# Masking the chosen feed-forward blocks by GpSimd with gates loaded over DRAM, in place of a selector product on TensorE

## What is computed

```python
prob = softmax(xf @ router_w.T + router_b)
_, idx = top_k(prob, 4)
mask = zeros((n, 16), bool).at[arange(n)[:, None], idx].set(True)
h = einsum('nd,ibd->nib', xf, w1b) + b1b
h = relu(where(mask[:, :, None], h, 0))
y = einsum('nib,dib->nd', where(mask[:, :, None], h, 0.0), w2b) + b2
```

## Time and profile before

| | us |
|---|---|
| median of 3 runs | 829.46 (828.54 to 829.77) |
| the profiled execution | 827.81 |
| its span | 826.0 |
| PE busy | 812.7 |
| DVE busy | 576.8 |
| ACT busy | 426.3 |
| POOL busy | 284.2 |

### The profile page before, as it was taken

The page is one execution under the profiler, slowest core; times in us unless marked ns, Lnnn a source line. Parts: engine busy times, 40 slices in busy tenths (PEclk is TensorE's granted clock), DMA queues, the critical chain, the costliest instruction groups (busy, mean ns, idle before and its releaser), DMA issues.

```text
span 826.0 us, 14866 instructions
## 1 busy us (share of the span) xinstructions
PE 812.7 (98%) x5275; PEld 490.6 (59%) x5275; DVE 576.8 (70%) x1785; ACT 426.3 (52%) x1018; POOL 284.2 (34%) x301
## 2 busy tenths in 40 slices
PE   7999999999999999999999999999999999999998
PEld 3677454544556655656666556664766556465764
DVE  6879787787998766675786866667676776767312
ACT  3523555564645645554564554645565454546552
POOL 4494249343650158067041028509400002000000
PEclk9999999999999999999999999999999999999999
DMA  8952515232514253240333215232070415000011
GB/s 266 275 163 78 168 54 166 93 90 92 166 61 136 80 143 142 65 122 19 100 121 76 93 53 166 91 91 92 3 216 2 116 54 142 15 15 16 15 58 52
DMA packets 53335, 81.91 MB, mean 99 GB/s; under 512 B 6796, under 2 KB 22092, under 8 KB 53260
## 3 DMA queue, kind: packets, MB, share of 16 engines
q1 hardware_dynamic: 53260, 80.95, 32.4%
HBM read 43.06 MB, written 37.88 MB: 98 GB/s over the span
## 4 chain that ended last, share of the span: by engine, by line
PE 92%; DVE 4%; ACT 2%; issue 1%; DMA 1%; SPq 0%; ACTq 0%; DVEq 0%
PE o_bank L1149 16%; PE banks L1074 15%; PE banks L1133 14%; PE banks L1049 14%; PE banks L1062 14%; PE banks L1023 7%; PE banks L1136 3%; PE banks L1032 3%; PE banks L1101 3%; PE banks L1053 2%; ACT probs L950 2%; DVE part_max L1342 1%; PE banks L1013 1%; DMA bqk_sb<-in_bk 1%; DVE o_norm L1379 1%
## 5 line engine op out<-in xcount | busy, mean ns | idle before, releaser
L950 ACT ACTIVATE probs<-banks 128x512 f32<-128x512 f32 (+3 forms) x768 | 328.0, 496 | 243.8 <-PE banks L1136 174.4
L1133 PE MATMUL banks<-q_st,k_st 99*128 99x512 bf16 (+3 forms) x768 | 234.8, 327 | 2.6 <-ACT probs L950 1.0
L1074 PE MATMUL banks<-k_st,q_st 96*128 96x512 bf16 (+3 forms) x768 | 228.7, 327 | 0.6 <-DVE part_max L1342 0.2
L1345 DVE CUSTOM_DVE_ANT_0 banks<-banks,tri,part_max 128x512 f32<-128x512 f32 (+3 forms) x256 | 128.9, 556 | 68.3 <-PE banks L1074 67.9
L1342 DVE TENSOR_REDUCE part_max<-banks 128x1 f32<-128x512 f32 x256 | 160.0, 677 | 17.6 <-PE banks L1074 17.2
L1345 DVE CUSTOM_DVE_ANT_0 banks<-banks,tri 128x512 f32<-128x512 f32 (+3 forms) x256 | 120.0, 515 | 34.4 <-PE banks L1074 33.5
L836 POOL TENSOR_SCALAR max_neg<-row_max 128x16 f32<-128x16 f32 x32 | 8.2, 255 | 382.1 <-DVE row_max L1345 382.1
L1049 PE MATMUL banks<-xnT,w_sb 128*128 128x256 f32 x512 | 134.5, 386 | 0.1
L1149 PE MATMUL o_bank<-probs,v_sb 128*17 128x512 f32 (+3 forms) x1536 | 133.2, 487 | 0.7 <-DVE o_norm L1379 0.7
L1062 PE MATMUL banks<-w_sb,hT 128*128 128x256 f32 x512 | 121.2, 382 | 0.0
L1074 PEld LDWEIGHTS banks<-k_st,q_st 96*128 96x128 bf16 x768 | 73.4, 98 | 73.6 <-issue 19.6
(11 more groups left out here) (100 smaller groups left out, 734.3 us busy)
## 6 DMA issues: line engine op xcount, KB each, us to landing
term_scratch<-pieces SPq DMA_DIRECT2D x84, 256.0 KB, 2.8
q_st<-term_scratch SPq DMA_DIRECT2D x16, 768.0 KB, 6.0
k_st<-term_scratch SPq DMA_DIRECT2D x16, 768.0 KB, 8.4
y_scratch<-o_norm SPq DMA_DIRECT2D x31, 256.0 KB, 2.1
acc<-in_x SPq DMA_DIRECT2D x8, 512.0 KB, 4.0
rope_sb<-y_scratch SPq DMA_DIRECT2D x15, 256.0 KB
out<-acc SPq DMA_DIRECT2D x7, 512.0 KB, 2.9
x_sb<-in_x SPq DMA_DIRECT2D x3, 1024.0 KB, 5.9
```

Of the source, the lines that this page charges most:

```text
L950: nc.scalar.activation(probs[:, h, PROBS_AT[u]:PROBS_AT[u] + w], filled("score", n, k, h)[:, 0:w], ACT.Exp, scale=SCALE).then_inc(s_out, 1)
L1074: nc.tensor.matmul(bank[:, 0:w], q_st[0:KROWS, at, h, i * P:(i + 1) * P], k_st[0:KROWS, at, h, c * HALF:c * HALF + w], start=True, stop=Tr ...
L1133: last = nc.tensor.matmul(bank[:, 0:w], k_st[0:SROWS, at, h, j * P:(j + 1) * P], q_st[0:SROWS, at, h, q0:q0 + w], start=True, stop=not dia ...
L1345: ins = nc.vector.tensor_tensor_reduce(bank[:, 0:w], bank[:, 0:w], tri[:, HALF - w:HALF], 1.0, least, ALU.add, ALU.max, to)
```

## The change

In row 0 nothing changes in kind: the selector product stays, with `sel` and the mask now on 16 partitions instead of 128. In rows 1 to 3 the third matmul of `hidden` is left out. The mask (now called `chosen`, 1 for a chosen block) is transposed by PE as before, copied by DVE to `chosenT`, stored to DRAM (`store_chosen`), and read back with every block's row repeated over the 64 partitions of its hidden values into `gates` (`load_gates`, two DMAs for a quarter, a buffer each for even and odd quarters). GpSimd multiplies `hT` by `gates` in place, two m at a time (`gate`), and PE's `ffn_tile` waits on `gated` for each pair instead of on ACT. `sel` now lies in the second buffer of `gates` and the last group's output weights `wo_last` in `x_sb`, loaded in row 3 by one DMA from a prepared input instead of four at the start. The planner gets a cost for the gate (2700 columns), puts gates right behind splits in its priority, counts a hidden unit of rows 1 to 3 as a quarter-column product less, and holds an `ffn` part back until it thinks the gates are done.

```diff
-COST = {"hid": 2 * 4 * QTR + QTR, "ffn": FB // 2 * 4 * D, "proj": KB * 4 * HALF, "v": KB * 4 * (D + NBLK),
+COST = {"hid": 2 * 4 * QTR, "masked": 2 * 4 * QTR + QTR, "ffn": FB // 2 * 4 * D, "proj": KB * 4 * HALF, "v": KB * 4 * (D + NBLK),
...
+GATED, GATES = 500, 20000
-            todo = min(able, key=lambda todo: todo[1][0] != "split")
+            todo = min(able, key=lambda todo: ("split", "gate").index(todo[1][0]) if todo[1][0] in ("split", "gate") else 2)
+    def work_ready(what):
+        return what[0] != "ffn" or what[1] == 0 or gated.get((what[1], what[2] // 2, 2 * what[3] + 1), clock + 1) <= clock
...
+            def store_chosen(b):
+                if b >= 3:
+                    for buffer in range(2):
+                        sp.wait_ge(gates_in[buffer], (b - 2) * 2 * 32)
+                sp.wait_ge(m_out, M_COUNT["chosenT", b])
+                sp.dma_start(gate_scratch[b % 2], chosenT[:]).then_inc(chosen_out, 16)
+            def load_gates(b, q):
+                if b == 1 and q == 1:
+                    sp.wait_ge(s_out, S_COUNT["hid", 0, 3, FB - 1])
+                elif b > 1 or q > 1:
+                    sp.wait_ge(gated, (b * 4 + q - 5) * FB // 2)
+                if q == 0:
+                    sp.wait_ge(chosen_out, b * 16)
+                tokens = slice(q * QTR, (q + 1) * QTR)
+                for i in range(2):
+                    rows = gate_scratch[b % 2].rearrange("(m i) t -> i m t", i=2)[i, :, tokens]
+                    sp.dma_start(gates[i * 64:(i + 1) * 64, q % 2], rows.partition_broadcast(64)).then_inc(
+                        gates_in[q % 2], 16)
...
                 load_stacks(n + 2)
                 if b:
+                    store_chosen(b)
                     store_y(n - 1, 1)
                     load_y(b - 1, 1, 2, 4)
+                    load_gates(b, 0)
+                    load_gates(b, 1)
                 store_y(n, 0)
...
                 place_maxima(n + 1, 1)
+                if b:
+                    load_gates(b, 2)
                 store_y(n, 1)
...
                 place_maxima(n + 2, 1)
+                if b:
+                    load_gates(b, 3)
                 store_y(n + 1, 1)
...
+            def gate(b, q, pair):
+                pool.wait_ge(s_out, S_COUNT["hid", b, q, 2 * pair + 1])
+                if pair == 0:
+                    pool.wait_ge(gates_in[q % 2], (b * 2 + q // 2 - 1) * 32)
+                blocks = slice(2 * pair, 2 * pair + 2)
+                nc.gpsimd.tensor_tensor(hT[:, blocks, :], hT[:, blocks, :], gates[:, q % 2, blocks, :],
+                                        ALU.mult).then_inc(gated, 1)
...
-                nc.tensor.matmul(bank[:, 0:QTR], sel[:, m, :], unselT[:, tokens], start=False,
-                                 stop=True).then_inc(s_fill, 1)
+                if b == 0:
+                    if q == 0 and m == 0:
+                        pe.wait_ge(m_out, M_COUNT["chosenT", 0])
+                    last = nc.tensor.matmul(bank[:, 0:QTR], sel[:, m, :], chosenT[:, tokens], start=False, stop=True)
+                last.then_inc(s_fill, 1)
...
-                    if t % 2 == 0:
+                    if t % 2 == 0 and b == 0:
                         pe.wait_ge(s_out, S_COUNT["hid", b, t // 2, m])
+                    elif t % 2 == 0 and m % 2 == 0:
+                        pe.wait_ge(gated, (b * 4 + t // 2 - 4) * FB // 2 + m // 2 + 1)
```

More of the change, by code:

```diff
@@ L207 @@
 SPLIT, PLACE = 1200, 16000
-POOL = {"split": 3600, "sin": 5640, "cos": 5640, "add": 5640, "high": 2500, "rest": 5100, "mid": 2500,
+GATED, GATES = 500, 20000
+POOL = {"gate": 2700, "split": 3600, "sin": 5640, "cos": 5640, "add": 5640, "high": 2500, "rest": 5100, "mid": 2500,
         "low": 5100, "xn": 1580, "bias": 5700}
@@ L229, in arrange @@
     to_turn = [(n, half) for n in range(GROUPS) for half in range(2)]
+    gates = {}
     wide, values_free = True, 0
-    pool, pool_todo, pool_free, split = [], [], 0, {}
+    pool, pool_todo, pool_free, split, gated = [], [], 0, {}, {}
     def pool_work(ready, *works):
@@ L247, in pump @@
                 split[todo[1][1:]] = pool_free + SPLIT
+            elif todo[1][0] == "gate":
+                gated[todo[1][1:]] = pool_free + GATED
     def engine_of(kind):
@@ L317, in do_work @@
         what = works.pop(0)
+        while not work_ready(what):
+            clock += 50
+            pump()
         order.append(what)
@@ L324, in do_work @@
                 do_max()
-            order.append(works.pop(0))
+            what = works.pop(0)
+            while not work_ready(what):
+                clock += 50
+                pump()
+            order.append(what)
             clock += COST["ffn"]
             read(what, at, READ["ffn"])
+            wide = True
             return 2 * COST["ffn"]
-        read(what, fill(what, COST[what[0]]), READ[what[0]])
+        read(what, fill(what, cost(what)), READ[what[0]])
+        if what[0] == "chosenT":
+            gates[what[1]] = ready["vector"] + GATES
+        elif what[0] == "hid" and what[1] and what[3] % 2:
+            pool_work(max(ready["scalar"], gates.get(what[1], 0)), ("gate", what[1], what[2], what[3] // 2))
         if what[0] == "out" and what[1] + 1 < B and what[2] % 2:
@@ L336, in do_work @@
             chores.append((ready["scalar"] + FREED, scored + 9, ("found", what[1])))
-        return COST[what[0]]
+        return cost(what)
     def chore_ready():
@@ L393, in arrange @@
             do_max()
-        elif works:
+        elif works and work_ready(works[0]):
             do_work(works)
@@ L403, in arrange @@
             chores.extend((clock, scored + 2 * j + 2, what) for j, what in enumerate(steps))
-        total, done = sum(COST[what[0]] for what in works + [what for _, what in later]), 0
+        total, done = sum(cost(what) for what in works + [what for _, what in later]), 0
         for i in range(NU * GH):
@@ L421, in arrange @@
                     do_run()
-                elif may_work and done + COST[works[0][0]] / 2 <= share - SPARE:
+                elif may_work and done + cost(works[0]) / 2 <= share - SPARE:
                     if not wide and wide_max_ready():
@@ L490, in block_kernel @@
         tri_k = tri[:, HALF - P:HALF]
-        sel = sb("sel", [P, FB, P], BF16)
+        gates = sb("gates", [P, 2, FB, QTR], BF16)
         pieces = sb("pieces", [P, 2, NPIECE, T], BF16)
@@ L499, in block_kernel @@
         yT = rope_sb[:, 0]
-        wo_last = sb("wo_last", [P, D])
+        wo_last = x_sb[:, 0, :]
+        sel = gates[0:NBLK, 1, 0:FB // 2, :].rearrange("p a (c m) -> p (a c) m", m=P)
         o_norm = sb("o_norm", [P, 2, HALF])
@@ L877, in _ @@
             for what in POOL_ORDER:
-                if what[0] == "split":
+                if what[0] == "gate":
+                    gate(*what[1:])
+                elif what[0] == "split":
                     split_maxima(*what[1:])
@@ L1183, in _ @@
                     pe.wait_ge(wv_in, 32)
-                if what == ("unselT", 0):
+                if what == ("chosenT", 0):
                     pe.wait_ge(mask_in, 48)
@@ L1411, in take @@
             def take(what):
-                if what[0] == "unselT":
-                    take_unselected(*what[1:])
+                if what[0] == "chosenT":
+                    take_chosen(*what[1:])
                 elif what[0] == "ffn":
@@ L1493, in constants @@
     tri[:, HALF - P:] = np.where(np.arange(P)[None, :] > np.arange(P)[:, None], -BIG, 0.0)
-    sel = np.zeros((P, FB, P), np.float32)
+    sel = np.zeros((NBLK, FB, P), np.float32)
     for m in range(FB):
```

106 lines of the change are left out of this document (56 added, 50 removed).

## The result

The changed kernel takes 830.25 us (830.05 to 830.54, 15 runs), the kernel before 828.38 us (827.75 to 829.77, 15 runs) beside it: a ratio of 1.0022 [1.0015, 1.0029]. It is slower by 0.2%, where 1.0% faster was forecast.

A forecast was written before the change was run, and what follows sets the result against it. PE was taken to pace the kernel, with 92% of the chain. 827.81 - 10.3 (products) + 1.1 (late gate) + 0.6 (shorter filler) = 819.2 us, plus 1.65 to the runs' median: 820.9 us, 1.0% faster; range 817.5 to 826.5.

The forecast's parts named there:

- The price of a product: PE, rows 1 to 3: each removed selector product holds PE about 0.107 us, so 96 save 10.3 us.
- Row 0 keeps its 32: Row 0's selector products: reading 16 partitions instead of 128 costs nothing, since the count of columns is the same.
- its weight load lies beside other matmuls: PE, selector product: its weight load overlaps other matmuls, so nothing was counted for it.
- Between nothing and half of the saving I take that 6%: 0.6 us: Evictions on DVE or ACT: with hidden units as shorter filler, 0.6 us of the saving is given back.
- rival (a): PE's saving turns into waits for evictions, the new order having less filler: half of 10.3 us goes, 825.4 us; chance 0.18.
- The order now keeps the same units: Between last hidden unit and tile: distances stay but for 0.1 to 0.3 us, so eleven tiles' gates cost nothing.
- The gates: GpSimd, 48 gates of 1.07 us (upper bound 1.18): PE waits once, row 1 quarter 3 pair 3, 1.1 us.
- rival (d): DVE slows beside GpSimd's gates, which read two SBUF operands: 26 us on DVE, half on the chain, 832 us; chance 0.03.
- Quarter 2's rotary steps: GpSimd, quarter 2: `add` and `high` stand ahead of pairs 2 and 3; gate 3 still ends about 1.4 us before its reader.
- The last tile of all: Smallest distance from ACT's write to the tile's read, 2.4 us; at least 0.7 us left after the gate.
- SyncE, the DMAs and the splits: Added loads and stores hidden, gates ahead of splits harmless: nothing counted; range allows 0 to 2 and 0 to 3 us.
- what would show it: Trace signs: 32 selector products, PE busy near 803 us, one `hT` wait; wrong if DVE and ACT's chain share grows over 1%.

## Why the prediction was wrong

In one line: 827.9 - 10.1 (96 products) + 4.3 (new order) + 1.5 (gates) + 6.6 (16 partitions in row 0) = 830.2 us. Each term is the difference of two kernels in this order; in another order the terms differ, as the gates in the old order do.

- **The price of a product: right.** 10.3 us were forecast for 96, 10.1 came out, and PE's busy time fell to 802.1 us in the kernel that only leaves them out ("near 803"). The chain in the earlier trace rows gave it, and the entry's 273 ns in the earlier trace rows would have misled.
- **"Row 0 keeps its 32; that they now read 16 partitions instead of 128 I cost at nothing, since the count of columns is the same": the step that failed most, by 6.6 us.** The count of columns is not all; a product of 16 or 64 rows between full ones costs 0.2 us more. The sentence ahead of it fails with it: "its weight load lies beside other matmuls" held for 128 partitions (it begins 0.214 us ahead of its product), not for the 16 of row 0 (0.004 us). The trace of before had the clue, outside the rows that I read: the last group's output product with 64 rows and its neighbour with 128 have means of 428 and 431 ns, while the same product among its like has 381. From start to start they take 0.31 to 0.32 us and their like 0.22, and at each change between 128 and 64 rows the first load leads its product by 0.002 us, the second by 0.213.

```profile
L1101 PE MATMUL banks<-wo_sb,rope_sb 128*128 128x256 f32 x112 | 26.7, 381 | 0.0
L1111 PE MATMUL banks<-wo_sb,rope_sb 128*128 128x256 f32 x8 | 2.8, 431 | 0.0
L1112 PE MATMUL banks<-wo_sb,rope_sb 64*128 64x256 f32 x8 | 2.8, 428 | 0.0
```

- **"Between nothing and half of the saving I take that 6%: 0.6 us": the term mis-sized, 4.3 us in its place.** The mechanism of rival (a) came, at 0.4 of the saving, but not for "less filler" (the old order has as little and gives up none of the 10.1 us): the order that the planner laid anew is the worse one. "The order now keeps the same units" is true between the last hidden unit and the tile, where I had compared it; nothing was said of the rest of the order, and there the loss lies.
- **The gates: 1.5 us against 1.1, stretch right, most of the cause wrong; that the sizes are near each other is luck.** The duration, 1.158 us, lay between 1.07 and the upper bound of 1.18. PE waits for `hT` once, in row 1 quarter 3, and at no other tile; but that wait is 0.4 us where about 1 was forecast, and making the gate punctual gives only 0.25. The time comes from rival (d)'s mechanism, DVE held by a gate, at 0.9 us instead of 13. I had ruled it out by the fused maximum, which reads one operand from PSUM, and that still holds: in the changed kernel its form on 128x512 with `part_max` takes 753 ns beside a gate (21 times) and 751 ns with no long operation of GpSimd beside it (19 times). What was held are a copy, a maximum, a product and an addition within SBUF. The Trainium skill ("GPSIMD Engine Reference", section "Specifications"), which I cited, names instructions with two SBUF inputs or in a 2-port mode; I applied it only to the large operations. The maximum, the product and the addition have two SBUF inputs, and the trace agrees. The held copy has a single input, so by that rule it would be one in a 2-port mode, which no run here shows.
- **Quarter 2's rotary steps** leave gate 3 0.25 us in the new order (row 1: it ends at 392.53 us and PE reads at 392.78), not the 1.4 us that I wrote, and in the old order they make it late. It cost nothing here, by luck. The last tile of all, which I took for the tightest where GpSimd is free, kept 0.9 us (at least 0.7 forecast).
- **SyncE, the DMAs and the splits: right.** The loads of 256 KB land in 6.1 us, and no wait of PE ends with one or with `max_pc`. GpSimd waits for them three times (29.8 us) where nothing is due.

The base was off a little too: 829.46 us, the median of three runs, stands 1.1 us above the 828.38 of 15. It is small beside the miss.

The list under "what would show it" was half useful: PE's busy time, 813.0 against "near 803", shows the miss at once; the share of DVE and ACT in the chain did not grow (6% and 6%), since PE's waits are short and many.

## What to carry over

Before narrowing a product's partitions, look at what stands beside it: in these runs products padded with zero rows to 65 or 128 partitions cost nothing extra, and products on 64 or 16 partitions cost 0.2 us each time among full ones. When a change lets a planner lay the order anew, time the new order without the change as a case of its own; here keeping the old cost and moving three gates turned 0.2% slower into 1.2% faster. When GpSimd gets a tensor operation on two SBUF operands, list the small operations of VectorE within SBUF that stand on a path, copies and those with two inputs above all, not only the large ones.

## What the hardware showed that was not expected

- A bf16 product with 16 or 64 partitions between full float32 ones: +0.095 us ahead of it, +0.10 us on it, and +0.10 us on a float32 product directly behind; with 65 partitions none of these. Its weight load begins 0.004 us ahead of it instead of 0.214. Score products with 99 rows directly behind it lose next to nothing (0.220 to 0.226 us).
- A 128x32 copy or maximum on VectorE within SBUF took 1.13 us instead of 0.18 while GpSimd multiplied 128x512 in place, and ended with it; a 128x8 product took 0.84 instead of 0.16 us and a 128x128 addition 0.87 instead of 0.28. Match-and-replace operations beside such a multiplication kept their 0.16 us, and the fused maximum that reads PSUM its 0.75 us.
